# First layer: the comparisons and the edge addition read one of their two operands from PSUM

## The reference, cut to what matters

```
m     = relu(x[src] + edge_attr)                     # 400000 x 32
neigh = segment_sum(m, dst, 12500)
x1    = layernorm(x + (1 + eps) * x + neigh)         # first layer
out_deg, in_deg = clip(counts of src, 1), clip(counts of dst, 1)
y     = x1 * rsqrt(out_deg)
agg   = segment_sum(y[src], dst, 12500) * rsqrt(in_deg)
out   = layernorm(x1 + agg)                          # second layer
```

## Time and profile before

| what | us |
|---|---|
| median of three runs | 7740.76 |
| lowest and highest run | 7676.73, 7744.13 |
| span of the profiled execution, first to last instruction | 6639.4 |
| time of the profiled execution itself | not given beside its span |
| GpSimd busy | 5097.3 (77% of the span) |
| VectorE busy | 2830.9 (43%) |
| TensorE matmuls busy | 2745.6 (41%) |
| ScalarE busy | 1587.9 (24%) |

### The profile page before, as it was taken

How to read it: one execution, slowest core, us unless ns; L and a number is a source line. 1 busy time by engine, 2 the same in 40 slices (tenths; PEclk the granted TensorE clock), 3 DMA queues, 4 the chain that set the end, 5 groups by cost and what they waited for, 6 DMA issues and landing times. The chain is left out here.

```text
span 6639.4 us, 68329 instructions
## 1 busy us (share of the span) xinstructions
PE 2745.6 (41%) x22843; PEld 2293.6 (35%) x22843; DVE 2830.9 (43%) x4668; ACT 1587.9 (24%) x2158; POOL 5097.3 (77%) x4335
## 2 busy tenths in 40 slices
PE   2222222222222222222222222222278888888884
PEld 2222222222222222222222222222256667666664
DVE  5232332332322323323233233232467777777774
ACT  0000000000000000000000000000078888888883
POOL 7787787787877877877778777787677777777771
PEclk7555655655655556556555565555589999999997
DMA  1111111111111111111111111111011111111110
GB/s 44 24 21 21 24 21 21 24 21 22 24 21 24 21 22 24 21 22 24 21 24 21 22 24 21 24 21 22 13 41 18 18 19 19 18 19 19 18 18 23
DMA packets 246274, 147.86 MB, mean 22 GB/s; under 512 B 159872, under 2 KB 229073, under 8 KB 245713
## 3 DMA queue, kind: packets, MB, share of 16 engines
q0 software_dynamic: 138400, 80.97, 9.1%
q1 hardware_dynamic: 107850, 66.58, 4.0%
HBM read 141.61 MB, written 5.61 MB: 22 GB/s over the span
## 5 line engine op out<-in xcount | busy, mean ns | idle before, releaser
L151 POOL DMA_INDIRECT rows<-in_x,src_t x3125 | 3799.8, 1216 | 957.6 <-issue 952.0
L395 PE MATMUL agg<-dst_hot,msg 128*33 128x128 f32 x6250 | 947.5, 327 | 2488.8 <-ACT msg L379 2488.8
L395 PEld LDWEIGHTS agg<-dst_hot,msg 128*33 128x33 f32 x6250 | 835.6, 137 | 2594.4 <-ACT msg L379 2516.2
L151 POOL DMA_INDIRECT rows<-table,src x1200 | 1285.2, 1071 | 422.4 <-issue 380.2
L593 ACT ACTIVATE counts<-built 128x686 bf16<-128x686 f32 x1925 | 1452.5, 984 | 262.6 <-PE built L618 246.1
L379 ACT ACTIVATE msg<-edge_t 128x800 f32<-128x800 f32 (+1 forms) x126 | 108.9, 864 | 4607.7 <-DVE edge_t L315 4607.7
L315 DVE TENSOR_TENSOR edge_t<-edge_t,rows 128x800 f32<-128x800 f32 (+1 forms) x126 | 125.1, 993 | 2110.8 <-DMA rows<-in_x,src_t 2110.8
L618 PE MATMUL built<-key_hot,hi_hot 128*128 128x343 bf16 x3850 | 930.2, 325 | 106.8 <-ACT counts L593 56.1
L637 PE MATMUL applied<-counts,x_parts 128*96 128x175 bf16 x7546 | 913.7, 246 | 0.8 <-ACT prod L598 0.8
L637 PEld LDWEIGHTS applied<-counts,x_parts 128*96 128x96 bf16 x7546 | 786.4, 128 | 153.0 <-ACT counts L593 1.0
L391 PE MATMUL hist<-lo_hot,hi_hot 128*128 128x98 bf16 x3125 | 277.9, 283 | 1002.9 <-DVE lo_hot L306 1002.9
(11 more groups left out here) (109 smaller groups left out, 723.2 us busy)
## 6 DMA issues: line engine op xcount, KB each, us to landing
edge_t<-in_edge_attr SPq DMA_DIRECT2D x125, 400.0 KB
rows<-in_x,src_t POOLq DMA_INDIRECT x3125, 2.4
rows<-table,src POOLq DMA_INDIRECT x1200
src_t<-in_src SPq DMA_DIRECT2D x125, 12.5 KB
dst_t<-in_dst SPq DMA_DIRECT2D x125, 12.5 KB
base_t<-in_dst SPq DMA_DIRECT2D x125, 0.5 KB
x<-x SPq DMA_DIRECT2D x1, 1568.0 KB
x<-in_x SPq DMA_DIRECT2D x1, 1555.8 KB
```

The lines of the kernel that those rows point to most:

```text
L151: gp.indirect_dma_start(rows_d[:, j, :], None, nodes, bass.IndirectOffsetOnAxis(ap=src_d[:, j:j + 1].bitcast(U32), axis=0),).then_inc(s, 16)
L395: last = te.matmul(agg[:, :], msg[:, j, :], dst_hot[:, j, :], start=(j == 0), stop=(j == J - 1))
```

## The change

The row of integers is copied once to a bank of PSUM, and the three comparisons read it there. For each group ScalarE copies the edge features as loaded to two banks of PSUM; the addition reads them there, and the gathered rows in SBUF, and still writes `edge_t`. VectorE waits for that copy ahead of the addition, and ScalarE waits for the group's loads ahead of the copy. The other operand of each of the four operations stays in SBUF, as do all outputs.

```diff
@@ -230,6 +211,10 @@
                 turn = [pb(f"turn{k}") for k in range(2)]
                 misc = pb("misc")
 
+                iota_ps = pb("iota_ps")[:, 0:P]
+                edge_ps = own.enter_context(nc.psum_tensor("edge_ps", [P, 1024], F32))[:, 0:J * D].rearrange("p (j d) -> p j d", d=D)
+                s_edge = sem("s_edge")
+
                 VG = 10
                 PIECES = [(0, J - CH), (J - CH, J)]
 
@@ -241,6 +226,7 @@
                     def after(ins):
                         ve.wait_ge(s_v, V(ins))
                     V(ve.memset(x_0[:, :, :], 0.0))
+                    V(ve.tensor_copy(iota_ps, iota[:, :]))
                     V(ve.memset(msg[:, :, D:DE], 1.0))
                     V(ve.memset(acc[:, :], 0.0))
                     ve.wait_ge(s_prep, 64)
@@ -301,18 +287,19 @@
                             ve.tensor_scalar(s_hi[:, :], quot[:, :], ROUND, ROUND, ALU.add, ALU.subtract).then_inc(s_v, 1)
                             ve.wait_ge(s_v, v + 3)
                             ve.scalar_tensor_tensor(s_lo[:, :], s_hi[:, :], -float(C), src_t[:, slot, :], ALU.mult, ALU.add).then_inc(s_v, 1)
-                            ve.tensor_tensor(hi_hot[:, :, :], tiles_of(iota[:, :], J), last_dim(s_hi[:, :], P), ALU.is_equal).then_inc(s_v, 1)
+                            ve.tensor_tensor(hi_hot[:, :, :], tiles_of(iota_ps, J), last_dim(s_hi[:, :], P), ALU.is_equal).then_inc(s_v, 1)
                             ve.wait_ge(s_v, v + 4)
-                            ve.tensor_tensor(lo_hot[:, :, :], tiles_of(iota[:, :], J)[:, :, 0:C], last_dim(s_lo[:, :], C), ALU.is_equal).then_inc(s_v, 1)
-                            ve.tensor_tensor(dst_hot[:, :, :], tiles_of(iota[:, :], J), last_dim(rel[:, :], W), ALU.is_equal).then_inc(s_v, 1)
+                            ve.tensor_tensor(lo_hot[:, :, :], tiles_of(iota_ps, J)[:, :, 0:C], last_dim(s_lo[:, :], C), ALU.is_equal).then_inc(s_v, 1)
+                            ve.tensor_tensor(dst_hot[:, :, :], tiles_of(iota_ps, J), last_dim(rel[:, :], W), ALU.is_equal).then_inc(s_v, 1)
                             for j0, j1 in PIECES if is_last else [(0, J)]:
                                 if j0 == 0:
 
                                     ve.wait_ge(s_rows[slot], i * (16 * J) + 16 * j1)
                                 else:
                                     ve.wait_ge(s_late, 16 * (j1 - j0))
-                                piece = edge_t[:, slot, j0:j1, :]
-                                ve.tensor_tensor(piece, piece, rows[:, slot, j0:j1, :], ALU.add).then_inc(s_v, 1)
+                                if j0 == 0:
+                                    ve.wait_ge(s_edge, g + 1)
+                                ve.tensor_tensor(edge_t[:, slot, j0:j1, :], edge_ps[:, j0:j1, :], rows[:, slot, j0:j1, :], ALU.add).then_inc(s_v, 1)
                             ve.wait_ge(s_agg, g + 1)
                             window = acc[0:DE, bass.ds(base, W)]
                             ve.tensor_tensor(window, window, agg[:, :], ALU.add).then_inc(s_v, 1)
@@ -373,7 +360,13 @@
                             A(sc.activation((hi_all, key_all)[what][:, t:t + m, :],
                                             turn[k % 2][:, 0:m * NC].rearrange("p (t g) -> p t g", g=NC), ACT.Copy))
 
+                        def hold_edges(i, slot):
+                            sc.wait_ge(s_in[slot], (i + 1) * 64)
+                            sc.activation(edge_ps, edge_t[:, slot, :, :], ACT.Copy).then_inc(s_edge, 1)
+
                         def step(i, slot, g):
+
+                            hold_edges(i, slot)
                             for n, (j0, j1) in enumerate(PIECES if isinstance(g, int) else [(0, J)]):
                                 sc.wait_ge(s_v, g * VG + (v0 + 8 + n))
                                 sc.activation(msg[:, j0:j1, 0:D], edge_t[:, slot, j0:j1, :], ACT.Relu).then_inc(s_a, 1)
```

## The result

The changed kernel is slower: median 8429.52 us of 4 runs (8420.03 to 8434.02) against 7708.74 us of 4 (7641.92 to 7744.13), ratio 1.0945, 95% interval 1.0878 to 1.1013. The forecast was 6900 us.

The account below looks back on a forecast made before the run. GpSimd issuing 3125 first-layer gathers was taken as the bound. The span of 6639.4 us less 842 us of holds gives 5797 us; with 1101.4 us outside the span kept, 6900 us, range 6750 to 7000.

Parts of the forecast that it names:

- The holds: First layer: three comparisons and the addition stop holding GpSimd's gathers, 842 us less; all four freed, 72%.
- rivals B and C: First layer: B, only the addition still holds gathers, 6994 us, 5%; C, all four operations still do, 7741 us, 10%.
- The durations: First layer: from PSUM, comparisons L304 and L307 take 3.5 to 4.0 us each; ScalarE's copy takes 0.87 us.
- The 1.25 ns a value: VectorE's four operations: time per value with PSUM input, from two shorter operations; 12.1 us a group in all.
- rival D: First layer: the holds stay and the four operations also run longer from PSUM, 7920 us, 5%.
- Its limit of 26.9 us for the comparisons: First layer: with holds gone, slower comparisons cannot lose time until they take 26.9 us a group.
- GpSimd stays the bound.: First layer: at 31.2 us a group GpSimd still sets the pace; the other engines' chain needs 20.7 us.
- none of this reaches GpSimd: First layer: VectorE's added wait for ScalarE's copy, with the comparisons and matmuls behind it, costs GpSimd zero.
- The 1101.4 us kept as they are.: Whole kernel: the median's excess over the profiled span stays unchanged and is added to the new span of 5797 us.
- Rival A: Whole kernel: time outside the span scales with it because unprofiled executions run slower throughout, 6759 us, 8%.
- the 125 x 31.2 us of the forecast: First layer: each of 125 groups falls from 37.93 to 31.2 us, 25 gathers at 1.248 us.

Follow-up runs that it names:

- the first group: Four follow-up runs on one chip: both kernels again, and the change cut to the comparisons or to the addition; kernel before 7527.31 us.
- r7: Changed kernel, GpSimd clearing a spare tile for 2.2 us after gathers 8, 16 and 25 of each first-layer group: 7602.12 us.
- r18: Changed kernel with GpSimd pauses: first layer 1.8 us after gathers 12 and 25, second 0.45 us after 4, 8, 12: 6689.85 us, ratio 1.0056.
- r2: Changed kernel once more, no edit, on the same chip as the repeat of the kernel before: 8289.53 us.
- r3: Changed kernel with only the three comparisons reading PSUM; addition back on SBUF, ScalarE's copy gone: 8266.91 us.
- r10: Changed kernel with few long GpSimd pauses: first layer after gathers 12 and 25 (2.3 us each), second after 8 of 16: 7250.03 us.
- r15: Changed kernel with every first-layer gather replaced by a plain load of 128 rows issued by SyncE's queue: 5247.98 us.
- r11: Changed kernel with one of the 25 source-count matmuls per group, the other 24 left out: 8327.73 us.
- r8: Changed kernel with gathers of 64 rows instead of 128, same number of gathers: 8272.25 us.
- r5: Changed kernel with TensorE's first-layer loop over one group instead of two: 8212.95 us.
- r6: Kernel before with TensorE's first-layer loop over one group instead of two: 7570.92 us.
- r13: Changed kernel with GpSimd pauses: first layer 2.3 us after gathers 12 and 25, second 1.1 us after 4, 8, 12: 6976.14 us, ratio 0.9216.
- r1: Kernel before once more, no edit, traced on the first follow-up chip: 7501.78 us, span 7500.0.
- r14: Changed kernel with GpSimd pauses: first layer 1.1 us after gathers 12 and 25, second 1.8 us after 4, 8, 12: 7062.98 us, ratio 0.9328.
- r9: Changed kernel with short GpSimd pauses: first layer after gathers 8, 16, 25, second after 4, 8, 12 of 16, clears about 0.35 us: 7390.54 us.

## Why the prediction was wrong

- **The holds.** Right for the four operations. 842 us were to go; on the chip of the first group 778 went (3736.1 to 2958.2 us; some had gone there already, since late instructions move the comparisons into GpSimd's own waits). The forecast said 0.946 us a gather and 2957 us in all; it was 947 ns and 2957.9 us. An operation with one input in PSUM and one in SBUF holds nothing, so rivals B and C fell. The trace agrees with the Trainium skill (SBUF — State Buffer, Who interferes with whom) that one SBUF input, outside the 2-port perf modes, does not contend, and disagrees with its inference on descriptor generation, as the earlier trace rows did. The reading of the earlier trace rows was too simple, though. The gather of 5.10 us ends 1.85 us after L247 and not 0.82, and the next one takes 2.25 us. Beside them ran two operations with a single SBUF input:

```profile
28.25 1.82 DVE L248 TENSOR_SCALAR c_hi<-c_src 77x3200 f32<-77x3200 int32 x1
30.11 1.82 DVE L249 TENSOR_SCALAR c_hi<-c_hi 77x3200 f32<-77x3200 f32 x1
```

L249 ends at 31.93 and its gather at 32.75, 0.82 us later as with the comparisons. So a single SBUF input can hold a gather too, when the operation runs at 0.57 ns a value (1.82 us for 3200) instead of 1.09. The four operations of the change run at the slower rate, so this did not touch the forecast.
- **The durations.** Right at the lower end: L290 3492 ns, L302 975 ns, ScalarE's copy 823 ns. The 1.25 ns a value that I had derived from the earlier trace rows was too much; rival D rested on it and fell too. That the kernel got slower, as D said, is no merit of D: neither of its two reasons came true. Its limit of 26.9 us for the comparisons was also wrong, since with the holds gone the idle time is 10.5 us and not 17.2, which makes it 9.66 + 10.5 = 20.2 us.
- **"GpSimd stays the bound."** This step failed. I had counted 20.7 us from L315 to the end of L307 and a margin of 10.5 us a group, from a trace in which the other engines got on at full speed beside the gathers. Where the kernel was timed they do not: during an unbroken stream of gathers the same 50 matmuls take 56 us in the group shown, so the chain no longer fits beside 31.2 us and is paid in the open, 28.7 us for every second group, 1718 to 1782 us in all. The path is the one that the prediction had dismissed with "none of this reaches GpSimd": late matmuls hold back L305, that the next comparisons, addition and relu, and only the relu frees the slot for the loads that GpSimd waits for. The holds that the change removes had been the pauses in which the others caught up: r7 puts as much pause back by other means and comes to 7602.12 us, beside 7570.96 of the kernel before. No rival had this.
- **"The 1101.4 us kept as they are."** Failed too, and should have warned me: time and span of one execution differ by 2 us. The difference was the same stalls: in the first group's run of the kernel before the span is 861 us longer, 116 us in the first layer (4878 against 4762) and 745 behind it (2622 against 1877). Rival A had asked whether executions that are timed run slower throughout, but priced it as a factor; it is a mechanism, and its size depends on how dense the gathers are.
- **Where nothing stalls** the arithmetic holds as far as r18 shows it: its gathers take 2966.4 us, and with the 933.2 us of issue that stand between them without pauses (r2) the first layer would be 3900 us, the 125 x 31.2 us of the forecast. That is worked out; the changed kernel itself wasn't run on such a chip.

Shown: the stall comes from GpSimd's unbroken stream of indirect gathers (r3, r7, r10, r15), how far TensorE gets before it goes with the number of its instructions (r11), it does not depend on the bytes fetched (r8) or on TensorE's loop (r5, r6), and it is there on four chips and not on a fifth. Not shown: by what path, whether direct DMAs of GpSimd do it in long runs, and what differs between the chips. A rival is left untested that fits a limit by number of instructions as well as a late supply of instructions does: these executions were recorded, and the engines may have been held up in writing the records. On the fifth chip they were recorded too and nothing stalled, so recording alone isn't enough; an execution without it was not compared.

## What to carry to other kernels

Compare a trace's span with the times before anything else: if they are not the same, the trace is of another kind of execution, and margins read from it are not margins of the one that is timed. A stall that is removed from one engine may have been the pause in which others caught up; ask of each hold who runs better during it, and if the gain turns into waits elsewhere, put back a shorter pause where it costs least (r13: 8% faster than before, where removing all of them made it 9% slower). On a chip where nothing stalls such pauses win nothing (r18: ratio 1.0056).

## What the runs showed of the hardware

- In the changed kernel an unbroken stretch of gathers, 1.25 us apart, goes on for 62 us. Within it TensorE's matmuls go at full rate until about 20 us in (the earliest single late one of any stretch comes 11 us in). Then they come at multiples of 0.70 us, mostly one in 2.8 us, and other engines see signals late, 31 us in the row of r11. After the gathers end it takes another 8 to 10 us.
- In the second layer, where TensorE issues more, the first late matmul of a stretch comes 5 to 6 us in at the earliest (r1 and the changed kernel), and the layer takes 2383 us instead of 1667.
- Two pauses of 2.33 us among 25 gathers remove the late matmuls from the first layer (r10, r13), not the late signals; with three, the signals are late by less than 5 us (r7). Two of 1.20 (r14) or three of 0.45 (r9) leave late matmuls.
- An operation of VectorE with its first input in PSUM and its second in SBUF holds no gather (947 ns on average) and takes as long as with both in SBUF: 3492 ns against 3484 for 3200 values, 975 against 993 for 800.
- The granted clock is 0.78 in the second layer with stalls and 0.94 without (0.56 to 0.59 in the first layer either way), so part of the longer time is matmuls at the lower clock: L618 takes 347 ns instead of 325, and TensorE is busy 133 us longer of the 716.
